# A graph kernel's sparse passes: one float32 product per pair instead of three bf16 limb products

## What is computed

```python
def _gcn_conv(h, W, b, src, dst, norm):
    h = h @ W
    msg = h[src] * norm[:, None]
    out = jax.ops.segment_sum(msg, dst, num_segments=N)
    return out + b

h = _bn(_gcn_conv(x, W1, b1, src, dst, norm), g1, be1)
h = _bn(_gcn_conv(h, W2, b2, src, dst, norm), g2, be2)
h = _bn(_gcn_conv(h, W3, b3, src, dst, norm), g3, be3)
```

## Time and profile before

| | us |
|---|---|
| median of 3 timed runs | 5912.68 (5912.21 to 5920.03) |
| the profiled execution: span, first to last instruction | 6780.8 |
| tables of edges and node statistics | 0 to 86 |
| `first_table` | 86 to 136 |
| gathers of the three passes | 136.0 to 3897.2 |
| expert layer and what lies around it | 3900 to 5000 |
| gathers of the attention layer | 5000.2 to 6311.7 |
| last feed-forward | to 6780.8 |

### The profile page before, as it was taken

How to read it: one execution, slowest core, us unless ns; L and a number is a source line. 1 busy time by engine, 2 the same in 40 slices (tenths; PEclk the granted TensorE clock), 3 DMA queues, 4 the chain that set the end, 5 groups by cost and what they waited for, 6 DMA issues and landing times. The chain is left out here.

```text
span 6780.8 us, 99586 instructions
## 1 busy us (share of the span) xinstructions
PE 4554.4 (67%) x23514; PEld 3233.5 (48%) x23515; DVE 2948.5 (43%) x7590; ACT 2475.0 (36%) x6436; POOL 3449.9 (51%) x3591
## 2 busy tenths in 40 slices
PE   2666666646666665556666655999936666766799
PEld 1444444433333333333433355999934444544466
DVE  5333333333333333333333353333336676766745
ACT  3333333333333333333333332444434344434222
POOL 2666666656666665666666633222235665665101
PEclk7666666666556665665556657999967787777899
DMA  6666666656666665555555543222143333333201
GB/s 205 161 163 162 163 163 163 164 149 170 172 171 172 170 170 169 152 165 163 163 163 162 162 138 110 36 36 36 34 133 87 91 93 91 93 92 88 73 1 38
DMA packets 550732, 862.18 MB, mean 127 GB/s; under 512 B 210941, under 2 KB 398326, under 8 KB 550422
## 3 DMA queue, kind: packets, MB, share of 16 engines
q0 software_dynamic: 219840, 641.37, 35.6%
q1 hardware_dynamic: 330710, 218.97, 10.8%
HBM read 709.79 MB, written 150.21 MB: 127 GB/s over the span
## 5 line engine op out<-in xcount | busy, mean ns | idle before, releaser
L1042 POOL DMA_INDIRECT rows<-node_limbs,psrc x2496 | 2361.6, 946 | 1449.8 <-issue 559.5
L1318 PE MATMUL ps<-rows,hot 128*128 128x257 bf16 x7488 | 1660.5, 391 | 1214.4 <-issue 875.6
L1107 DVE TENSOR_TENSOR shared<-shared,ps 128x257 f32 x2496 | 1056.5, 423 | 2255.6 <-remote 1233.5
L1318 PEld LDWEIGHTS ps<-rows,hot 128*128 128x128 bf16 x7488 | 879.0, 131 | 1907.8 <-issue 1244.1
L2253 POOL DMA_INDIRECT rows<-attn_table,psrc x832 | 786.8, 946 | 605.4 <-PE ps L2560 237.1
L2560 PE MATMUL ps<-rows,hot 128*128 128x264 f32 x1664 | 637.4, 539 | 265.5 <-DVE rows L2354 96.3
L1232 ACT ACTIVATE away<-iota_f,pdl 128x128 f32<-128x128 f32 x2496 | 759.3, 387 | 93.3 <-remote 51.6
L2560 PEld LDWEIGHTS ps<-rows,hot 128*128 128x128 f32 x1664 | 408.7, 262 | 413.5 <-issue 189.5
L1889 POOL DMA_INDIRECT resid<-feat,slot_node x105 | 165.0, 1571 | 622.8 <-DVE feat L1904 620.0
L2375 DVE TENSOR_TENSOR sums<-sums,ps 128x264 f32 x832 | 356.9, 429 | 233.5 <-remote 131.5
L2006 PEld LDWEIGHTS ps<-feat 128*128 128x128 f32 x3360 | 392.9, 192 | 8.4 <-DVE feat L1933 2.4
(11 more groups left out here) (467 smaller groups left out, 5120.3 us busy)
## 6 DMA issues: line engine op xcount, KB each, us to landing
slot_rows<-blank SPq DMA_DIRECT2D x450, 130.0 KB
rows<-node_limbs,psrc POOLq DMA_INDIRECT x2496
feat<-in_edge_attr_dram SPq DMA_DIRECT2D x832, 32.0 KB
node_limbs<-limbs SPq DMA_DIRECT2D x99, 196.0 KB, 3.9
feat<-slot_rows SPq DMA_DIRECT2D x105, 130.0 KB
rows<-attn_table,psrc POOLq DMA_INDIRECT x832
node_limbs<-limbs SPq DMA_DIRECT2D x12, 784.0 KB, 3.6
w<-in_L_ffn_W_dram SPq DMA_DIRECT2D x8, 1024.0 KB
```

What stands on the lines that cost most here:

```text
L1042: g.indirect_dma_start(rows[:, n % RING, :], None, tables[k % 2], bass.IndirectOffsetOnAxis(ap=psrc[:, n:n + 1], axis=0)).then_inc(row_sem ...
L1107: v.tensor_tensor(row, row, ps[banks(k, i)[h * G + b]][:, 0:F + 1], ALU.add).then_inc(added.h, 1)
L1318: mm = pe.matmul(ps[cycle[s]][:, 0:F + 1], hot[:, 2 * half + h, b, :], rows[:, s, m * LIMB:m * LIMB + F + 1], start=(m == 0), stop=(m == 2))
```

## The change

Table rows become 257 float32 numbers, 1028 bytes. All splitting goes, in `first_table` and in the passes. The table is stored from `acc` itself: in `first_table` chunk by chunk as soon as its rows are set, in the passes after `t_ready`. `hot` is float32 and is made in place, and each pair takes one float32 product. The ring stays at 16 buffers, now with a name. The gathers, their waits, PSUM banks, the DVE adds and everything on PE but the pair products stay as they were.

```diff
-    LIMB = F + 2
-    TROW = 3 * LIMB + 10
-    tables = [dram(f"node_limbs{k}", [NPAD, TROW], BF16) for k in range(2)]
+    TROW = F + 1
+    tables = [dram(f"node_rows{k}", [NPAD, TROW]) for k in range(2)]
...
+                        if hi - lo > 1:
+                            both += 1
+                        sp.wait_ge(rows_set.h, both)
+                        sp.wait_ge(rows_scaled.h, n + 1)
+                        sp.dma_start(tables[0][lo * P:hi * P, :].rearrange("(d p) f -> p d f", p=P), acc[:, lo:hi, :]).then_inc(rows_kept.h, 16)
+                    sp.wait_ge(rows_kept.h, 16 * len(CHUNKS))
...
-            rows = sb("rows", [P, RING, TROW], BF16, ctx)
-            hot = sb("hot", [P, 4, G, P], BF16, ctx)
-            away = sb("away", [P, 2, G, P], F32, ctx)
+            rows = sb("rows", [P, RING, TROW], F32, ctx)
+            hot = sb("hot", [P, 4, G, P], F32, ctx)
...
-                        sp.wait_ge(limbs_set.h, k * NT + j + 1)
-                        sp.dma_start(tables[(k + 1) % 2][bass.ds(d * P, P), :], limbs[:]).then_inc(limbs_kept.h, 16)
+                        sp.wait_ge(t_ready.h, k * NT + j + 1)
+                        sp.dma_start(tables[(k + 1) % 2][bass.ds(d * P, P), :], rows_of(acc, d)).then_inc(table_kept.h, 16)
...
-                            op = a.activation(away[:, u % 2, b, :], iota_f[:], ACT.Abs, bias=pdl[:, bass.ds(cols * G + b, 1)], scale=-1.0)
+                            op = a.activation(hot[:, u, b, :], iota_f[:], ACT.Abs, bias=pdl[:, bass.ds(cols * G + b, 1)], scale=-1.0)
...
-                        a.activation(hot[:, u], away[:, u % 2], ACT.Relu, bias=ones[:, 0:1], scale=-1.0).then_inc(onehot_ready.h, 1)
+                        a.activation(hot[:, u], hot[:, u], ACT.Relu, bias=ones[:, 0:1], scale=-1.0).then_inc(onehot_ready.h, 1)
...
-                            for m in range(3):
-                                mm = pe.matmul(ps[cycle[s]][:, 0:F + 1], hot[:, 2 * half + h, b, :], rows[:, s, m * LIMB:m * LIMB + F + 1], start=(m == 0), stop=(m == 2))
-                            mm.then_inc(aggregated.h, 1)
+                            pe.matmul(ps[cycle[s]][:, 0:F + 1], hot[:, 2 * half + h, b, :], rows[:, slot, :], start=True, stop=True).then_inc(aggregated.h, 1)
```

More of the change, by code:

```diff
@@ L186, in _build @@
     v_step = sem("v_step")
-    row_sem = [sem(f"row_landed{s}") for s in range(2 * G)]
+    row_sem = [sem(f"row_landed{s}") for s in range(RING)]
     idx_ready = sem("idx_ready")
@@ L880, in first_table @@
             offset = sb("offset0", [P, NT], F32, ctx)
[L881 to L885, removed]
-            with nc.Block() as block:
[L887 to L891, removed]
+            scale_ready, rows_set, rows_scaled, rows_kept = sem("scale_ready"), sem("rows_set0"), sem("rows_scaled0"), sem("rows_kept0")
+            with nc.Block() as block:
                 @block.sync
                 def _(sp):
-                    sp.wait_ge(padded.h, 3)
+                    both = 0
                     for n, (lo, hi) in enumerate(CHUNKS):
[L897 to L900, removed]
+                        if hi - lo > 1:
[4 more added lines that the diff above has]
+                    sp.wait_ge(rows_kept.h, 16 * len(CHUNKS))
                 @block.vector
@@ L906, in _ @@
                     v.scalar_tensor_tensor(offset[:], x_mean[:], -1.0, scale[:], ALU.mult, ALU.mult).then_inc(scale_ready.h, 1)
-                    def rows(n):
-                        lo, hi = CHUNKS[n]
+                    v.drain()
+                    for lo, hi in CHUNKS:
                         for d in range(lo + (hi - lo) // 2, hi):
@@ L957, in middle @@
-                    def middle(n):
-                        lo, hi = CHUNKS[n]
-                        a.wait_ge(rest_set.h, n + 1)
-                        a.activation(limbs[:, n % KEPT, 0:hi - lo, LIMB:LIMB + F + 1], rest[:, n % 2, 0:hi - lo, :], ACT.Copy).then_inc(middle_set.h, 1)
-                    a.wait_ge(scale_ready.h, 1)
-                    rows(0)
[L964 to L967, removed]
-                        middle(n)
@@ L1144, in iteration @@
                         if j is not None:
-                            d = take(k, j)
+                            take(k, j)
                         add_pairs(k, i, 0, tiles, range(0, G))
-                        if j is not None and k < 2:
-                            split(k, j, d)
                         tiles = node_tiles_of(v, 2 * i + 1)
-                        add_pairs(k, i, 1, tiles, range(0, G // 2))
-                        if j is not None and k < 2:
-                            finish(k, j)
-                        add_pairs(k, i, 1, tiles, range(G // 2, G))
+                        add_pairs(k, i, 1, tiles, range(0, G))
                         if j is not None:
@@ L1269, in iteration @@
                     def iteration(k, i, half, j):
-                        if j is not None and k < 2:
-                            high(k, j)
                         if k < 2 or not isinstance(i, int) or i < ITERS - 1:
```

88 lines of the change are left out of this document (16 added, 72 removed).

## The result

| | before | after |
|---|---|---|
| median, us | 5913.55 (5912.21 to 5920.03, 4 runs) | 5853.21 (5851.77 to 5853.53, 4 runs) |
| ratio, 95% interval | | 0.9899 (0.9887 to 0.9911) |
| forecast, us | | 5888, range 5845 to 5945 |

The sign and the range were right, the size was not: -60.3 us where -24.3 was forecast.

What follows compares the result with a forecast made beforehand. POOL's gather pace was taken to bound both loops, so only serial parts would move: first table -22.4, between passes -3.8, ends of passes +1.9, sum -24.3 from 5912.7 to 5888 us, range 5845 to 5945.

Steps and rivals of the forecast that it cites:

- Timed runs walk through both loops at POOL's pace: Passes and attention loop: gathers start 1.246 us apart in timed runs; short waits for PE belong only to the profiled execution.
- the sum: Profiled span 6780.8 less loop excesses 607.6 and 250.6 gives 5922.6 us, 10 us from the timed median.
- In the loops: 0: Passes and attention loop: POOL's gather pace stays 1.246 us and covers PE, DVE, ACT and DMA changes; 0 us.
- The first table, -22: Head: stores become the bound and the first gather starts at 113.6 instead of 136.0 us; -22.4 us.
- Between passes, -4: Two joints: the last tile's chain to the store loses 1.92 us each time; -3.8 us.
- the ends of the passes, +2: End of each of three passes: PE's perhaps three remaining pairs cost 0.21 us more each; +1.9 us.
- Inside the passes, 0: Iterations of the three passes: heavier products and lighter gathers stay hidden under POOL's pace; 0 us.
- Rival 1: `aggregate` in pass 0: PE becomes the pace if its clock falls towards 0.50; +57 us, 5945; chance 0.18.
- Rival 3: Head: 1028-byte rows store and gather badly, so the serial gain does not come; 5912, half-way 5900 us; chance 0.12.
- Rival 2: Loops gain too, half a microsecond per iteration on 104 iterations with splitting; another -50 us, 5838; chance 0.12.
- The reading of the bound is wrong if timed runs move by more than 35 us either way while the head and the joints move as said: Whole kernel: the forecast's own test of its claim that POOL's pace sets both loops; threshold 35 us.

Runs made afterwards that it cites:

- before_b: The kernel before, unedited, run and profiled again: 5912.1 us, profile span 5909.8 us.
- experiment 3: Empty instructions ahead of VectorE's attention loop: changed kernel with 59, 0.9944, with 21, 0.9968; kernel before with 197, 0.9954, with 5, 0.9998 (ratios to kernel before).
- after_again: The changed kernel, unedited, run again: 6708.4 us beside 6766.6 for the kernel before, ratio 0.9912.
- before_again: The kernel before, unedited, run and profiled again: 6780.5 us beside 6781.0.
- experiment 7: Kernel before with only the high limb's product: 6888.1 us beside 6781.0; changed kernel with every product issued twice: 6752.2 us where the changed kernel had 6708.4.
- after_b: The changed kernel, unedited, run and profiled again: 5857.2 us beside 5912.1 for the kernel before, ratio 0.9909.
- twice_c: Third run of the changed kernel with every product of the passes issued twice: 6691.1 us beside 6709.2 for the kernel before, ratio 0.9971.

## Why the forecast was right in sign and wrong in size

**"Timed runs walk through both loops at POOL's pace": right for the passes, for a wrong reason.** The passes of before_b take 3148.8 us, the sum had 3153.6; part of that closeness is luck, since the stop of 6.9 us at the start is absent, the joints are 15 us shorter, and a gather follows the one before in 1.251 us (median), some later, not in 1.246, which adds 17. But the waits for PE in the trace that I read were real time of a level at which TensorE stands still for 875.6 us before the products; profiling adds nothing to speak of (5909.8 against 5912.1).

**The step that failed: "In the loops: 0" for the attention loop.** It was put at nothing and gave -23.8 us. It rested on the sum that closed within 10 us, from which I took that the loop walks at POOL's pace and has no stop of its own but one. That the sum closed was luck, for it had two large errors of opposite sign: against before_b the attention loop was put at 1060.9 and takes 1088.9 (+28.0), and the stretch between passes and attention at 1103.0 and takes 1068.9 (-34.1). The longest stop of 25.8 us that I kept is not there at the short level; eleven smaller ones that I struck out as excess are. They stood in the trace before the change too, as a wait of VectorE:

```profile
DVE rows L2354 <- issue: 30.6, 11, 3.2
```

Eleven times, always at the loop's first instruction, with no releaser: by experiment 3 that is how the program's place shows, and the row was to be had before the forecast. With it the forecast would have carried a term of -24, 0 or, with longer stops, +13, depending on where the loop came to lie. I read POOL's and PE's waits and not VectorE's "issue" rows.

**The first table, -22: right.** First gather at 114.7, forecast 113.6. The stores, issued from 89.2 on, are the bound, as forecast:

```profile
88.12 11.90 ACT L909 ACTIVATE shared<-feat,offset,scale 128x256 f32<-128x256 f32 x24 [8.35 <-DVE offset L896]
...
89.24 16.50 SPq L889 DMA_DIRECT2D node_rows<-shared  x13
```

ACT needs 11.9 us (13.1 forecast). From the first store at 89.24 to the first gather at 114.65, less 1.5 for the barrier, are 23.9 us for what I had put at 23.8 by the store of x. The nine other profiles with the changed first table and no fill have 24.5 to 27.2. The Trainium skill's rule on rows that start off a block (DMA: Bandwidth & Descriptors, How a descriptor splits into AXI transactions) had given 26.8, an estimate; the spread holds both values and does not decide between them. The start before was 134.1 instead of 136.0, so the gain was 19.4.

**Between passes, -4: right, and the ends of the passes, +2: the wrong way.** The two stops, after:

```profile
1163.94 0.94 POOL L980 DMA_INDIRECT rows<-node_rows,psrc  x1 [9.01 <-DMA node_rows<-shared]
...
2213.44 0.94 POOL L980 DMA_INDIRECT rows<-node_rows,psrc  x1 [9.47 <-DMA node_rows<-shared]
```

They were 11.5 and 12.1 us in before_b, not 21.5 and 17.2: 2.5 and 2.7 less, where the forecast had 1.9 less for the splitting and 0.6 more for PE's last pairs. VectorE's end of pass 0, before_b:

```profile
1181.66 0.35 DVE L1118 TENSOR_SCALAR shared<-done_tile,dinv 128x257 f32 x1
...
1183.50 0.43 DVE L1127 TENSOR_TENSOR limbs<-rest,limbs 128x257 bf16<-128x257 f32 x1 [0.48 <-ACT limbs L1246]
```

and after:

```profile
1160.92 0.35 DVE L1056 TENSOR_SCALAR shared<-done_tile,dinv 128x257 f32 x1
```

The 1.92 us between the last tile's scaling and its last subtraction are gone, as said. From the end of the scaling (before, of that subtraction) to the next gather it takes 0.3 and 0.6 us more (2.67 and 2.92 for 2.36 and 2.37). From the start of the last gather to the end of the scaling, where the heavier products should have cost 0.6, it takes 0.9 and 1.3 less (7.28 and 7.49 for 8.18 and 8.78); what shortens that was not tested.

**Inside the passes, 0: nearly.** They lost 6.0, of which 5.1 in the middle one. In before_b 38 gathers of that pass start late, by 5.7 us together, most of them behind a longer gather that is the twelfth of its sixteen:

```profile
1481.07 1.20 POOL L1042 DMA_INDIRECT rows<-node_limbs,psrc  x1 [0.30 <-issue]
```

All four short-level profiles with the old passes have 1044.2 to 1045.0 in the middle pass, all four with the new ones 1038.9 to 1039.2. What makes those gathers longer stays open.

**The rivals.** Rival 1 (PE becomes the pace): at the short level no pass grew, and the clock in pass 0 rose with the heavier products, as the forecast had allowed. (At the long level pass 0 took 1268.5 in after_again and 1256.1 in before_again, the other two passes 9 to 15 less; the two are of different sessions, which leaves it open.) The first 1000 us of the passes (columns as in experiment 7), before_b:

```profile
150.00:1150.00 1000.00, 748.42 (x4102) 503.85 (x4103) 437.79 (x1181) 471.54 (x1257) 756.24 (x801) 0.74 0.75 197
```

and after_b:

```profile
150.00:1150.00 1000.00, 757.15 (x3272) 532.83 (x3271) 404.69 (x1088) 437.74 (x1149) 756.40 (x800) 0.89 0.57 138
```

PE is busy 76% of that time where it was 75%, with the clock at 0.89 for 0.74, and POOL's 756 us are the same: its pace did not move. Rival 3 (the serial gain does not come) is out by the head. Rival 2 named the size (-50) and the wrong place and cause: it asked for a gain in the iterations with splitting, and those gave under 6. "The reading of the bound is wrong if timed runs move by more than 35 us either way while the head and the joints move as said" was the right alarm: they moved by 60.

## What to carry over

An edit ahead of a long loop (here 354 instructions on VectorE) can move the time by tens of microseconds through the loop's place alone; before crediting or blaming an edit, look for stops with no releaser at the loop's first instruction, counted as often as the loop turns, and shift the loop with empty instructions as a control. A sum that closes on the measured time supports its terms only if each term is checked against something of its own: here +28 and -34 closed it. And when profile and timed runs differ by 15%, profile the old kernel again before calling the difference an artefact.

## What was not expected of the hardware

- A stop of 2.8 to 3.2 us (mean) on VectorE at every turn of a loop of 354 instructions, or none, by the loop's place in the program: none at 3041 and 3297, 30 to 35 us in 11 turns at 3062, 3080, 3100 and 3105.
- TensorE stood still before the products 439 times for nothing shown in an execution of 6787 us, and 33 times in one of 5910 us, of the same kernel; one chip showed both kinds. What decides it stays open.
- At the long level, a third of the products made the kernel before 107 us slower (clock 0.50 to 0.54 in two stretches of the passes), and doubling them cost the changed kernel 44 us (clock 0.93 to 0.95, in twice_c).
- At the long level a gather of 1568 bytes a row costs what one of 1028 does: 3751.2 us against 3749.7 from the first to the last of 2496.
